# A decoder layer over 32 sequences: two copies issued by ScalarE instead of SyncE, and the first sequence's preparation placed inside the context phase

## What is computed

```python
x = layernorm(x + self_attention(x))            # qkv = x @ w_qkv + b_qkv, 16 heads of 16, causal softmax, @ w_proj + b_proj
x = layernorm(x + cross_attention(x, ctx, ctx)) # q = x @ w_q, k = ctx @ w_k, v = ctx @ w_v, 16 heads of 64, @ w_o
h = concat([x, -x])
h = relu(s0 * (h @ sign(k0))) * 2
h = relu(s1 * (h @ sign(k1))) * 2
x = layernorm(x + s2 * (h @ sign(k2)))
```

## Time and profile before

| | us |
|---|---|
| median of 3 runs (lowest, highest) | 2479.45 (2477.03, 2479.72) |
| the profiled execution's own time | 2479.52 |
| its span in the trace | 2477.8 |
| end of the context phase's products on TensorE | 220.1 |
| first `scores_by_key` of the first sequence | 273.7 |
| mean granted TensorE clock | 0.963 |

### The profile page before, as it was taken

How to read it: one execution, slowest core, us unless ns; L and a number is a source line. 1 busy time by engine, 2 the same in 40 slices (tenths; PEclk the granted TensorE clock), 3 DMA queues, 4 the chain that set the end, 5 groups by cost and what they waited for, 6 DMA issues and landing times.

```text
span 2477.8 us, 54581 instructions
## 1 busy us (share of the span) xinstructions
PE 2187.5 (88%) x18572; PEld 1905.6 (77%) x18572; DVE 1480.1 (60%) x4548; ACT 1129.9 (46%) x2568; POOL 686.1 (28%) x847
## 2 busy tenths in 40 slices
PE   7996479898988998899889888988999989889897
PEld 6886368787777777787777777877888777778786
DVE  4452356666666666666666666666666666666664
ACT  5543244444444444444444544444444444444452
POOL 1000123323333232333233332222333333322331
PEclk9998699999999999999999999999999999999999
DMA  8887332233233333322332333333223333333310
GB/s 252 280 283 192 68 65 53 52 64 62 44 68 68 68 68 68 63 54 54 63 61 46 68 68 68 68 68 68 55 54 57 68 50 57 68 68 68 68 39 9
DMA packets 205156, 196.58 MB, mean 79 GB/s; under 512 B 50130, under 2 KB 184306, under 8 KB 205042
## 3 DMA queue, kind: packets, MB, share of 16 engines
q1 hardware_dynamic: 205108, 195.94, 38.1%
HBM read 69.37 MB, written 58.87 MB: 52 GB/s over the span
## 4 chain that ended last, share of the span: by engine, by line
PE 65%; DVE 9%; DMA 8%; issue 6%; SPq 5%; ACT 5%; DVEq 1%; ACTq 0%; POOL 0%; POOLq 0%
PE ps L1158 10%; PE ps L1335 9%; PE ps L1198 9%; PE ps L1199 8%; DMA q<-q 6%; PE ps L1303 4%; SPq L387 3%; PE ps L1167 3%; PE ps L1319 3%; PE ps L1139 2%; DVE q L863 2%; PE ps L1108 2%; ACT p2r L612 2%; PE ps L1234 2%; PE ps L1122 2%
## 5 line engine op out<-in xcount | busy, mean ns | idle before, releaser
L1198 PE MATMUL ps<-r_h,w 128*128 128x256 f16 x2048 | 483.1, 281 | 105.8 <-DVE r_l L822 105.8
L1199 PE MATMUL ps<-r_l,w 128*128 128x256 f16 x2048 | 479.9, 279 | 0.0
L836 DVE CUSTOM_DVE_ANT_0 junk<-ps,causal 128x128 bf16<-128x128 f32 (+1 forms) x1024 | 329.8, 356 | 176.9 <-PE ps L1223 173.7
L1198 PEld LDWEIGHTS ps<-r_h,w 128*128 128x128 f16 x2048 | 205.9, 101 | 149.2 <-DVE r_l L822 115.2
L487 POOL TENSOR_SCALAR_AFFINE_SELECT probs<-probs 128x512 f32<-128x512 f32 x256 | 163.4, 638 | 465.2 <-ACT probs L637 463.6
L576 ACT ACTIVATE r_h<-ps 128x512 f16<-128x512 f32 x256 | 152.5, 596 | 303.0 <-PE ps L1199 272.9
L612 ACT ACTIVATE p2r<-ps,low 128x77 f32<-128x77 f32 x1024 | 247.5, 343 | 60.7 <-DVE low L875 59.3
L501 POOL TENSOR_TENSOR p<-p2r,inv 128x308 f32<-128x308 f32 x256 | 194.6, 778 | 269.9 <-DVE inv L886 267.4
L637 ACT ACTIVATE probs<-ps 128x768 f32<-128x768 f32 x256 | 204.6, 812 | 109.5 <-PE ps L1234 109.4
L511 POOL TENSOR_SCALAR var_eps<-mv 128x2 f32<-128x2 f32 x96 | 20.9, 217 | 785.4 <-DVE mv L811 785.4
L1335 PE MATMUL ps<-vo_h,p2t 128*128 128x256 f32 (+1 forms) x1280 | 234.3, 290 | 2.5 <-DVE p2t L893 2.4
(11 more groups left out here) (145 smaller groups left out, 4860.3 us busy)
## 6 DMA issues: line engine op xcount, KB each, us to landing
vo_scratch<-vo_out SPq DMA_DIRECT2D x80, 448.0 KB, 4.7
vo<-vo_scratch SPq DMA_DIRECT2D x64, 512.0 KB
q_st<-p2t SPq DMA_DIRECT2D x192, 128.0 KB
k_bd<-p2t SPq DMA_DIRECT2D x192, 128.0 KB, 6.9
q<-q SPq DMA_DIRECT2D x128, 128.0 KB, 4.0
k_bd<-k_scratch SPq DMA_DIRECT2D x64, 154.0 KB, 3.6
x_in<-in_x SPq DMA_DIRECT2D x32, 256.0 KB, 2.7
out<-y SPq DMA_DIRECT2D x32, 256.0 KB, 3.1
```

Source lines behind the costliest of these rows:

```text
L836: dve.tensor_tensor_reduce(out=junk[:, e, b * P:b * P + width], in0=ps[:, 2 + b, e * width:(e + 1) * width], in1=causal[:, (1 - b) * P:], ...
L1198: pe.matmul(dst, w1[:, kk, m * P:(m + 1) * P], r0_h[:, kk, :], start=kk == 0, stop=False)
L1199: last = pe.matmul(dst, w1[:, kk, m * P:(m + 1) * P], r0_l[:, kk, :], start=False, stop=kk == KF - 1)
```

## The change

Four things are altered.

1. The two packing DMAs of each half leave SyncE's queue. ScalarE's `self_output` issues them itself, right behind the copy to `o_raw`, after waiting for that copy to end.
2. In each sequence's call the order is altered. On TensorE `scores_by_key(i, 2)` comes before `scores_by_query(i, 7)`, and `layer0(1)` before the second half of the next sequence's `queries_keys`. The projection stands behind 7 instead of 4 `layer1` pieces and the transposes of the normed rows behind 14 instead of 13. On VectorE `relu_low` of units 2 and 3 each come one step earlier, the last ahead of the second half's division.
3. The first sequence's preparation is put between the steps of groups 4 and 5 of the context phase, in banks 0 and 1: the load behind the saves of step (4, 1), the transposes in (4, 2), queries and keys in (4, 3) and (4, 4), values in (4, 5), the stacks on SyncE behind the saves of (4, 5), score pairs 0 to 4 in (5, 0) to (5, 4), the transposed maxima in (5, 5), pairs 5 and 6 in (5, 6) and (5, 7), pair 7 behind the last product.
4. SyncE's wait for all saves of the context phase moves from ahead of the first load to ahead of the first sequence's load of keys.

```diff
@@ SyncE @@
             def attention(i, g, first=False, more=True):
                 if more:
                     load(i + 1)
-                if not first:
+                if first:
+                    for n in range(4):
+                        sp.wait_ge(k_saved[n], 16 * (KX * NG // 4))
+                    for n in range(2):
+                        for c in range(2):
+                            sp.wait_ge(vo_saved[n][c], 16 * (KX * NG // 2))
+                else:
                     sp.wait_ge(pe_s2, nth(i, KX, 0))
                 load_keys(i)
...
                 stack_max(i, 1)
 
-                output_packed(i, 0)
                 if more:
                     query_stacks(i + 1)
-                output_packed(i, 1)
-                if more:
                     key_stacks(i + 1)
...
                     save_keys(g, j)
+                    if (g, j) == (4, 1):
+                        sp.wait_ge(w_bin, 4)
+                        sp.dma_start(x_in[:], x[0].rearrange("(b p) d -> p b d", p=P)).then_inc(x_loaded, 16)
+                    if (g, j) == (4, 5):
+                        sp.wait_ge(zero_saved, 16)
+                        query_stacks(0)
+                        key_stacks(0)
+                    if (g, j) == (5, 5):
+                        stack_max(0, 0)
@@ ScalarE @@
                 act.activation(o_raw[:, 2 * m:2 * m + 2, :], ps[:, 2, :], ACT.Copy).then_inc(a_o, 1)
+                act.wait_ge(a_o, nth(i, 2, m + 1))
+                act.dma_start(s_c[:, m, :], o_raw[1::2, 2 * m:2 * m + 2, :]).then_inc(s_packed[m], 16)
+                act.dma_start(o_c[:, m, :], o_raw[0::2, 2 * m:2 * m + 2, :]).then_inc(o_packed[m], 16)
...
+                    if (g, j) == (4, 2):
+                        transposed_x(0, 0)
+                    if (g, j) == (4, 3):
+                        act.wait_ge(small_in, 16 * 10)
+                        queries_keys(0, 0, 1)
+                    if (g, j) == (4, 4):
+                        queries_keys(0, 1, 0)
+                    if (g, j) == (5, 5):
+                        negated_max(0, 0, (0, S))
@@ VectorE @@
                 if not first:
                     relu_low(1, r0_h, r0_l, a_r0, d_r0, f, 1)
+                    relu_low(0, r0_h, r0_l, a_r0, d_r0, f, 2)
                 self_output_low(i, 0)
                 if not first:
-                    relu_low(0, r0_h, r0_l, a_r0, d_r0, f, 2)
+                    relu_low(1, r0_h, r0_l, a_r0, d_r0, f, 3)
                 self_output(i, 1)
-                if not first:
-                    relu_low(1, r0_h, r0_l, a_r0, d_r0, f, 3)
                 self_output_low(i, 1)
...
+                    if g == 5 and j != 5:
+                        self_max(0, j - (j > 5), 0)
@@ TensorE @@
-            Z_PJ, Z_LN, Z_XT = 4, 13, 16
+            Z_PJ, Z_LN, Z_XT = 7, 14, 16
...
                 filler2(0)
+                scores_by_key(i, 2)
                 if f is not None:
                     scores_by_query(i, 7)
-                scores_by_key(i, 2)
...
                 scores_by_key(i, 6)
+                filler0(1)
                 if more:
                     queries_keys(i + 1, 1)
                 scores_by_key(i, 7)
-                filler0(1)
...
+                    if (g, j) == (4, 2):
+                        pe.wait_ge(a_ct, NG)
+                        pe.wait_ge(d_ct, NG)
+                        transposed_inputs(0, 0)
...
+                    if (g, j) == (5, 0):
+                        pe.wait_ge(const_pool, N_CONST)
+                        pe.wait_ge(d_v, 1)
+                        pe.wait_ge(q_stacked, 112)
+                        pe.wait_ge(k_stacked, 96)
...
+                    if g == 5 and j != 5:
+                        scores_by_query(0, j - (j > 5), 0)
             value_outputs(NG - 1, KX - 1)
...
+            scores_by_query(0, NP - 1, 0)
+            pe.wait_ge(a_k2, KX * NG)
+            pe.wait_ge(a_vp, KX * NG)
+            pe.wait_ge(d_vp, KX * NG)
             pe.wait_ge(w_low[4], 1)
             pe.wait_ge(w_bin, 5)
             attention(0, None, None)
```

More of the change, by code:

```diff
@@ L1055, in _ @@
             value_outputs_out(NG - 1, KX - 1)
[L1056 to L1062 removed]
+            self_max(0, NP - 1, 0)
             attention(0, True, None, None)
```

195 lines of the change are left out of this document (89 added, 106 removed).

## The result

| | before | after |
|---|---|---|
| median of 4 runs (lowest to highest), us | 2479.37 (2477.03 to 2479.72) | 2412.76 (2411.45 to 2413.74) |
| ratio to before, 95% interval | | 0.9733 (0.9716 to 0.9750) |
| span of the profiled execution | 2477.8 | 2411.0 |
| mean granted TensorE clock | 0.963 | 0.977 |
| first `scores_by_key` of sequence 0 | 273.72 | 235.47 |

The change gains 66.6 us. The forecast was 87.

A forecast was written before the change was run, and what follows sets the result against it. TensorE was taken as the bound except where it waits on transfers: layer1's stall in the loop and the first sequence's preparation. 2479.5 - 33 (first sequence) - 54 (1.8 us over 30 sequences) = 2392.5, range 2350 to 2450.

The forecast's parts named there:

- the new wait: Loop, second half: ScalarE's issues delay relu of unit 1, so layer0(6) starts 2.0 us later and TensorE idles 2.7.
- What the issues cost: Loop, ScalarE: each packing DMA issue takes 0.61 us with the gap, between 0.05 and 1.2.
- R1: Rival: ScalarE's second pair of issues queues behind SyncE's, 1.2 us each; 2446, or 2420 if partly waited for; 27%.
- R2: Rival: the issue is nearly free on ScalarE, layer0(6) stays near 1043.5, the clock stays up; 2348 us; 12%.
- The packing off the path: Loop, second half: packing lands at 1047.5, before relu_low of unit 3 is done at 1047.7, so it leaves the path.
- Gain 2.5 us: Loop, behind the projection: cross queries start at 1057.6 for 1060.15, a gain per sequence before the clock's loss.
- The clock's term: Loop, behind layer0(6): the low clock costs 1.4 us in half the sequences, 0.7 on average, leaving 1.8 gained.
- The 2414: Whole kernel: the time forecast if idle times of 2.7 us always bring the low clock.
- The first sequence: Preparation moved into the context phase: 33 us gained together, from 25 to 38; first scores_by_key at 238.9 for 273.7.
- The wait for the key stacks at (5, 0): Context phase: stacks are ready at 207.9, TensorE arrives at 201.8 and idles 6.1 us.
- The rule on queues: Skill rule on the first sequence's packing: issuing from several engines saves only issuing time, making its +2 us +1.
- the 2 that I gave the first packing: First sequence: its own packing, with earlier issue and free path and no filler above it, gains 2 us.

The follow-up runs named there:

- e3: The changed kernel with the loop of before (packings on SyncE, old order and piece numbers), keeping the first sequence's preparation in the context phase; 2446.59 us.
- e7: The changed kernel with the four packing DMAs of a sequence back on SyncE's queue; 2406.33 us.
- e8: e7 with 18 added matmuls per sequence, results unread, in TensorE's idle time ahead of the projection; 2385.85 us.
- e9: e8 with the second half's packing issued ahead of the two last query stacks in SyncE's queue; 2373.69 us.
- e5b: The changed kernel with unit 1's relu ahead of ScalarE's second copy and its relu_low ahead of VectorE's first division; 2431.94 us.
- e1: The kernel before with only the four packing DMAs of a sequence moved to ScalarE's queue; 2453.39 us.
- e10: The changed kernel with 20 unread matmuls ahead of layer0(6) and each ScalarE packing DMA split into two halves of the partitions; 2588.74 us.
- e2: The kernel before with the new order and piece numbers on TensorE and VectorE, packings still on SyncE; 2438.18 us.

## Why the prediction was right, and where it was not

The direction and the range held: 2412.76 lies in 2350 to 2450, 20.8 above the forecast. Of the mechanism, the new wait and the falling clock held; that the packing leaves the path, and that the queue and the order gain at the full clock, did not.

- **What the issues cost.** I took 0.61 by SyncE's row; the rows show 0.54 and, in the second half, 0.80. R1, that ScalarE's issues queue behind SyncE's, is there in this form: the last issue takes 0.2 us more beside SyncE's stacks than the 0.63 of the first half. It isn't the doubling that it supposed. The section that R1 names in the Trainium skill ("Perfetto Trace Analysis", "DMA Instruction — HWDGE (DVE, Sync)") says in a note under its diagram that the pair that issues such DMAs is SyncE and ScalarE; I gave only the VectorE and SyncE of its title, so it spoke for R1 more than I let it. R2 is out.
- **The new wait.** By the working `relu` of unit 1 starts 2.1 us behind the copy (1041.9 to 1044.0; the last part's 2.7 counted from the old copy), and 2.11 was measured. `layer0(6)` was foreseen 2.0 later with 2.7 of idle; it is 1.9 later with 2.6. `values(3)` was foreseen with 1.2 of idle and has 0.8.
- **The packing off the path.** Foreseen free, with landing at 1047.5 ahead of VectorE's turn, by the old 4.9 us from issue to landing. It takes 5.8. In the sequence shown the division still waits 0.47 for it, and TensorE 0.60 for the division's low part. In the dip-free sequences it is still on the path to the projection, which comes 23.56 us behind the input's transposes; by the forecast it would be 23.1 (1051.0 less the 1027.9 of those transposes), and before it was 22.99.
- **"Gain 2.5 us": the term that was too large.** The old way from the projection to the transposes was measured in a sequence whose clock had fallen, 1051.08 to 1058.49 or 7.4 us, and the new one was worked out at the full clock. By my own price of a low stretch, 1.4 us, that left 1.1 for the queue and the order. A dip-free sequence of the same trace was not looked at. There that way takes 5.78:

```profile
1392.04 0.47 PE L1167 MATMUL ps<-wp_h,o_h 128*128 128x256 f32 x2
...
1397.82 0.60 PE L1147 MATMUL ps<-ident,x 128*128 128x128 f32 x4
...
1399.48 0.48 PE L1158 MATMUL ps<-xt_h,wq_h 128*128 128x256 f32 x2
```

  This sequence starts at 1369.02, so the cross queries came at 30.46 us; the dip-free ones now have 30.43 on average, where 29.7 was forecast. The queue and the order together give 0.02 us a sequence in place of 1.1, and the clock gives 1.70 in place of 1.4. A dip-free sequence now takes 66.41, 1.72 less than the 68.13 of a dipped one before; 0.78 of the 2.5 isn't there.
- **The clock's term.** "Half of the sequences, 0.7 on average" was right in the count (15 of 28) and double in the price: 0.60 each or 0.32 on average, since the idle time ahead of the projection takes up a part. The count was a choice between never and always that no row gave, so that it came true was luck. And two of 28 sequences of before had nothing to win, 0.12 on average. So 1.72 - 0.32 - 0.12 = 1.28 us a sequence where 1.8 was forecast: 16 us over 30 sequences. With the last sequences, which lost 1.4 us against before, and the second one, which gained 0.3, the loop and its end gave 34.7 and not 54. The 2414 that I gave for a clock that always falls is near the measured time by chance: it fell in half.
- **The first sequence.** The wait for the key stacks at (5, 0): 6.1 foreseen, 6.16 measured.

```profile
204.51 0.55 PE L1227 MATMUL ps<-k_bd,q_st 128*128 128x256 f32 x1 [6.16 <-DMA k_bd<-p2t]
...
249.97 2.08 PE L1239 MATMUL ps<-q_st,k_bd 128*128 128x256 f32 x8 [3.91 <-DMA q_st<-neg_max]
```

  The first `scores_by_key` came at 235.47, foreseen 238.9; 2.6 us of the 3.4 were there ahead of the change's first instruction. The fifth came 14.5 behind the first and not 12.7. Together 32.1 for 33, of which those 2.6 are not the change's; e3, by its median, gained 30.7.
- **The rule on queues** would have taken 1 us off the 2 that I gave the first packing. The traces show none of the 2: from the first sequence's transposes to the second's the changed kernel takes 140.6 us, and e3, e7, e8 and e9 with their packings on SyncE take 137.4 to 140.9. e9 and e7 say that the rule was right for the loop too, where I hadn't applied it.

What stays open: what picks the sequences in which the clock falls. Idle times of one length, 2.6 us, brought it in 15 of 28 sequences of the changed kernel, 21 of e5b and 17 of e1, often in every second one, and the 3.3 us of e10 in 13 of 28, where the 3.5 us of before brought it in 26.

## What to carry to other kernels

Look in the trace for the same loop step with and without the low clock before pricing a stall: a gain that shows only against the dipped one is the clock's, and the cheapest way to it may be work that nobody needs, put into the idle time (28 spare matmuls in each sequence gained 40 us). An idle time that can't be removed belongs where the work behind it has slack. And a transfer that was late behind others wasn't helped by another engine's queue here, but by being issued ahead of two of them; the issue then also stays off an engine that computes.

## What the runs showed of the hardware

- An idle time of TensorE of 1.9 to 2.8 us was followed by the half clock in half to three quarters of the sequences (e7 14 of 28, the changed kernel and e2 15, e1 17, e5b 21), for 3.4 us each time; one of about 3.5 in 26 of 28 before and 25 in e3, but one of about 3.3 in 13 of 28 in e10. The 1.30 us that stayed ahead of `layer0(6)` in e8 and e9 brought none in 28 sequences each.
- The same low stretch costs from 0 (e1, behind `layer0(6)`) over 0.60 (changed) and 1.4 (e2, e5b) to 1.70 us (before), by what waits behind it.
- Of two DMA issues of 128 KB in a row ScalarE's first takes 0.53 to 0.55 us, the second 0.63 in the first half and 0.80 in the second, where SyncE issues beside it. Halves of 64 partitions take as long to issue, and the division that waits for them starts 2.9 us later.
- The same packing landed 2.1 us behind its issue with no stack on the way (first half), 3.9 behind four 128 KB stacks (e9), 4.8 to 4.9 behind six, and 5.8 behind six when ScalarE issued it and key stacks came beside it.
